# Gated experts summed in one running sum that VectorE finishes, with VectorE's step reordered and one norm fused

## What is computed

```python
# 1: top-k cross attention to a context (257 x 192), then a state-space layer and an MLP
scores = einsum(x @ Wq, ctx @ Wk) / sqrt(DH)          # 4 heads
topv, topi = top_k(scores, 32); attn = scatter(softmax(topv)); attn_mean = attn.mean(heads)
c_t = attn_mean @ (ctx @ Wv)
xf  = layernorm(x) * (1 + g * scale_in(c_t)) + g * shift_in(c_t)
y   = s4d(xf) * (1 + g * scale_out(c_t)) + g * shift_out(c_t)   # a long convolution
xt  = x + y
xt  = xt + gelu(layernorm(xt) @ W1 + b1) @ W2 + b2
x1  = x + layernorm(xt)
# 2: attention over the 32 rows
x2  = x1 + attention(layernorm(x1))
# 3: eight experts, top 2 of them gated
logits = cos_scores(h, centroids) + h @ w_route.T
gates  = softmax(top 2 of logits)
out    = x2 + sum_e gates[e] * (gelu(h @ w1[e] + b1[e]) @ w2[e]) + gates @ b2
```

## Time and profile before

| | |
|---|---|
| median of 3 runs | 602.14 us (600.91 to 603.63) |
| profiled execution, its own time | 601.02 us |
| its span, first to last instruction | 599.2 us |
| mean granted clock of PE | 0.972 |
| busy: PE, DVE, ACT, POOL | 550.1, 497.5, 292.6, 282.3 us |
| steps with all four tiles in work | some 31.6 us each |

### The profile page before, as it was taken

One profiled execution on the slowest core, in us unless ns is written; L12 is line 12 of the kernel. 1 busy time (PEld: TensorE's weight loads), 2 busy tenths in 40 slices (PEclk: granted clock), 3 DMA queues, 4 the chain that ended last, 5 costly groups with the idle time before them and its releaser, 6 DMA issues.

```text
span 599.2 us, 13091 instructions
## 1 busy us (share of the span) xinstructions
PE 550.1 (92%) x4558; PEld 406.0 (68%) x4558; DVE 497.5 (83%) x1761; ACT 292.6 (49%) x768; POOL 282.3 (47%) x662
## 2 busy tenths in 40 slices
PE   2588487999999999999999999999999999989877
PEld 2344264868686877778786868686868687766755
DVE  7997877689898999989899999898999899966433
ACT  3132242364646565555546463646464656434522
POOL 7755147525445362626363636353544535251621
PEclk9998898899999999999999999999999999989988
DMA  8488203030403030301213030303030300000000
GB/s 269 76 311 340 79 1 122 2 113 2 131 2 131 1 128 4 100 33 59 73 25 108 19 113 20 112 19 114 2 131 2 131 1 10 2 10 2 9 1 18
DMA packets 17957, 42.33 MB, mean 71 GB/s; under 512 B 2770, under 2 KB 9570, under 8 KB 17380
## 3 DMA queue, kind: packets, MB, share of 16 engines
q1 hardware_dynamic: 17892, 41.51, 20.7%
HBM read 39.37 MB, written 2.13 MB: 69 GB/s over the span
## 4 chain that ended last, share of the span: by engine, by line
PE 77%; DVE 3%; issue 3%; POOL 3%; ACT 2%; POOLq 0%; DVEq 0%
PE D L1136 9%; PE BB L1136 9%; PE BB L1159 8%; PE D L1153 8%; PE SS L1116 4%; PE SS L1122 3%; PE PC L1277 3%; PE PC L1316 2%; PE PC L1279 2%; PE BB L1237 2%; PE BB L1238 2%; PE BB L1272 2%; PE BB L1271 2%; PE PC L1219 2%; PE BB L1254 2%
## 5 line engine op out<-in xcount | busy, mean ns | idle before, releaser
L553 POOL TENSOR_SCALAR var_in<-mv 128x1 f32<-128x1 f32 x64 | 14.0, 219 | 238.4 <-DVE mv L782 140.9
L817 DVE MATCH_REPLACE8 work<-top,work 128x257 f32<-128x257 f32 x192 | 77.5, 412 | 0.0
L1136 PE MATMUL D<-ang,e_w 128*128 128x128 f32 x512 | 73.6, 292 | 0.0
L1136 PEld LDWEIGHTS D<-ang,e_w 128*128 128x128 f32 x512 | 65.6, 202 | 10.1 <-issue 10.1
L811 DVE MAX8 top<-work 128x8 f32<-128x257 f32 x192 | 71.1, 412 | 0.0
L1153 PE MATMUL D<-expw,ang 128*128 128x256 f32 x256 | 66.0, 389 | 1.2 <-ACT ang L628 0.9
L1136 PE MATMUL BB<-ang,w 128*128 128x128 f32 x512 | 65.0, 282 | 0.9 <-ACT ang L709 0.9
L1136 PEld LDWEIGHTS BB<-ang,w 128*128 128x128 f32 x512 | 62.1, 196 | 3.1 <-ACT ang L709 1.3
L628 ACT ACTIVATE ang<-BB,cols 128x128 f32<-128x128 f32 x128 | 36.5, 367 | 50.9 <-PE BB L1136 50.9
L1159 PE MATMUL BB<-expw,ang 128*128 128x256 f32 x256 | 57.9, 379 | 0.0
L649 ACT ACTIVATE expo<-SS,nmax,srs 128x257 f32<-128x257 f32 x64 | 32.7, 562 | 51.5 <-DVE work L797 51.3
(11 more groups left out here) (262 smaller groups left out, 1238.5 us busy)
## 6 DMA issues: line engine op xcount, KB each, us to landing
ctx_n<-in_ctx_n SPq DMA_DIRECT2D x16, 768.0 KB, 4.3
ctx_t<-in_ctxT SPq DMA_DIRECT2D x16, 514.0 KB
ctx_t<-in_ctxT SPq DMA_DIRECT2D x16, 257.0 KB
xT<-in_xT SPq DMA_DIRECT2D x16, 128.0 KB, 2.5
x_all<-in_x SPq DMA_DIRECT2D x4, 512.0 KB, 9.2
out<-out_sb SPq DMA_DIRECT2D x16, 128.0 KB, 1.7
ctx_l<-in_ctx_l SPq DMA_DIRECT2D x16, 96.0 KB, 5.1
w<-in_W SPq DMA_DIRECT2D x1, 1024.0 KB
```

The costliest lines, as they stand in the source:

```text
L817: V.match_replace(work[:, 2 * q + k, :], top[:, 2 * q + k, 8 * r8:8 * r8 + 8], work[:, 2 * q + k, :], TAKEN).then_inc(chains["taken"], 1)
L1136: ins = MM(bank[:, 128 * m:128 * m + 128], w[:, k, at:at + 128], xs[:, 128 * k:128 * k + 128], start=k == 0, stop=k == 1)
```

## The change

- `acc` is one buffer. Addition 0 adds the first product to x2, additions 1 to 7 add to `acc`, each of them waiting for the one before, and addition 8 writes `out_sb` itself, after a wait for the store that read it last. GpSimd's addition and its semaphore are gone; SP's store waits for DVE's ninth addition.
- The norm of tile c is two instructions: `u_c = (xt2 - mean) * g`, placed before rstd is there, and `x1 = u_c * rstd + xb_c`.
- On DVE many dependent instructions that stood next to each other now have an instruction of another tile between them. `find8`, `take8` and `probs` are split so that their halves can stand apart, and the nine gated additions stand one by one. PE's and ACT's programs are unchanged.

```diff
-        acc = [over("ang", D) for _ in range(2)]
+        acc = over("ang", D)
...
-                    wait(sp, s["fin_g"], dd.count(1, 1))
+                    wait(sp, s["acc_v"], dd.count(NE + 1, NE + 1))
...
-                if dd:
-
-                    wait(pool, s["acc_v"], dd.count(NE + 1, NE + 1))
-                    wait(pool, st_out[dd.p], dd.half(16, 0))
-                    nc.gpsimd.tensor_tensor(out_sb[dd.p][:, :], acc[0][:, :], acc[1][:, :], ALU.add).then_inc(s["fin_g"], 1)
...
+                        else:
+                            wait(dve, s["acc_v"], dd.count(NE + 1, k))
+                        if k < NE:
+                            so_far = acc if k else x2[dd.p]
+                            V.scalar_tensor_tensor(acc[:, :], bank, gate[:, k:k + 1], so_far[:, :], ALU.mult, ALU.add).then_inc(s["acc_v"], 1)
+                        else:
+                            wait(dve, st_out[dd.p], dd.half(16, 0))
+                            V.tensor_tensor(out_sb[dd.p][:, :], bank, acc[:, :], ALU.add).then_inc(s["acc_v"], 1)
...
+                if c:
+                    wait(dve, s["st1_v"], one(c))
+                    V.scalar_tensor_tensor(u_c[:, :], xt2[:, :], mv[1][:, 0:1], gout[:, :], ALU.subtract, ALU.mult).then_inc(chains["u"], 1)
...
+                    V.scalar_tensor_tensor(x1[:, :], u_c[:, :], rstd[1][:, 0:1], xb_c[:, :], ALU.mult, ALU.add).then_inc(s["x1_v"], 1)
...
                 if dd:
-                    gated(range(0, 2))
-                if a:
-                    take8(a, 0, 2)
-                if b:
-
+                    gated((0,))
+                if a:
+                    take8(a, 0, 2, (1,))
+                if dd:
+                    gated((1,))
+                if b:
                     wait(dve, s["y_a"], one(b))
                     wait(dve, s["y_mm"], one(b))
...
+                    V.tensor_tensor(yb[:, :], yb[:, :], B1[:, 0:D], ALU.mult).then_inc(chains["y"], 1)
+                if a:
+                    find8(a, 0, 3, (0,))
+                if b:
+                    wait(dve, chains["y"], b.count(2, 1))
+                    V.tensor_tensor(yb[:, :], yb[:, :], B1[:, D:2 * D], ALU.add).then_inc(chains["y"], 1)
+                if a:
+                    find8(a, 0, 3, (1,))
+                if b:
+                    wait(dve, chains["y"], b.count(2, 2))
                     wait(dve, s["xln_g"], one(b))
                     V.tensor_tensor(xt[:, :], yb[:, :], xln[b.n % 3][:, :], ALU.add).then_inc(s["xt_v"], 1)
+                if dd:
+                    gated((2,))
+                if b:
                     wait(dve, s["xt_v"], one(b))
                     link(V.bn_stats(bn[0][:, :], xt[:, :]))
                     V.bn_aggr(mv[0][:, :], bn[0][:, :]).then_inc(s["st0_v"], 1)
-                if a:
-                    find8(a, 0, 3)
...
                 if dd:
-                    gated(range(2, 4))
+                    gated((3,))
...
                 if dd:
-                    gated(range(4, 6))
+                    gated((4,))
                 if a:
                     take8(a, 0, 3)
+                if dd:
+                    gated((5,))
+                if a:
+                    find8(a, 1, 1)
                 if c:
                     wait(dve, s["o2_mm"], one(c))
                     V.tensor_tensor(x2[c.p][:, :], x1[:, :], C0[:, 0:D], ALU.add).then_inc(s["x2_v"], 1)
```

More of the change, by code:

```diff
@@ L274, in build @@
                  "xb_g x1_v st2_v rs2_g xl2_v xT2_mm xT2_a v_mm v_a s_mm nmaxc_v pc_a pt_v r_mm r_a o2_mm x2_v st3_v rs3_g inorm_g "
-                 "xl3_v xT3_mm xT3_a lg_mm dots_a nbest_v ed_a gate_v gT_mm gT_a e1a_mm e1b_mm g2a_a g2b_a eo_mm acc_v fin_g").split()
+                 "xl3_v xT3_mm xT3_a lg_mm dots_a nbest_v ed_a gate_v gT_mm gT_a e1a_mm e1b_mm g2a_a g2b_a eo_mm acc_v").split()
         s = {n: sem(n) for n in names}
-        chains = {n: sem("self_" + n) for n in "tm g0 g1 g2 g3 len top taken u xhat best".split()}
+        chains = {n: sem("self_" + n) for n in "tm g0 g1 g2 g3 len top taken u xhat best y gate bn2 bn3".split()}
         ld_x = [sem(f"ld_x{k}") for k in range(4)]
@@ L802, in top8, with find8 @@
                 take8(a, q, r8)
-            def find8(a, q, r8):
-                for k in range(2):
+            def find8(a, q, r8, ks=(0, 1)):
+                for k in ks:
                     if r8 == 1:
@@ L865, in step @@
                     V.tensor_tensor(xt2[:, :], xt_b[:, :], B1[:, 0:D], ALU.add).then_inc(s["xt2_v"], 1)
+                if b:
+                    sums(b, 1)
+                if c:
                     wait(dve, s["xt2_v"], one(c))
-                    stats(1, xt2[:, :], c, "st1_v")
+                    link(V.bn_stats(bn[1][:, :], xt2[:, :]))
+                    V.bn_aggr(mv[1][:, :], bn[1][:, :]).then_inc(s["st1_v"], 1)
                 if a and a.n == 3:
@@ L970, in step @@
                     V.tensor_tensor(x2[c.p][:, :], x1[:, :], C0[:, 0:D], ALU.add).then_inc(s["x2_v"], 1)
+                if a:
+                    prob_of(a, 0, 0)
+                if c:
                     wait(dve, s["x2_v"], one(c))
-                    stats(3, x2[c.p][:, :], c, "st3_v")
+                    V.bn_stats(bn[3][:, :], x2[c.p][:, :]).then_inc(chains["bn3"], 1)
                 if a:
-                    probs(a, 0)
-                    top8(a, 1, 1)
+                    prob_of(a, 0, 1)
+                if c:
+                    wait(dve, chains["bn3"], one(c))
+                    V.bn_aggr(mv[3][:, :], bn[3][:, :]).then_inc(s["st3_v"], 1)
+                if a:
+                    sums(a, 0)
                 if dd:
-                    gated(range(6, 8))
+                    gated((6,))
                 if a:
-                    top8(a, 1, 2)
+                    take8(a, 1, 1)
                 if dd:
-                    gated(range(8, NE + 1))
+                    gated((7,))
+                if a:
+                    find8(a, 1, 2)
+                if dd:
+                    gated((8,))
+                if a:
+                    take8(a, 1, 2)
                 if a and a.n == 1:
```

80 lines of the change are left out of this document (41 added, 39 removed).

## The result

| | before | changed |
|---|---|---|
| median, and range | 602.88 us (600.91 to 605.47, 4 runs) | 634.57 us (633.91 to 635.39, 4 runs) |
| profiled execution | 601.02 us | 633.91 us |
| its span | 599.2 us | 632.1 us |
| mean granted clock | 0.972 | 0.957 |

The ratio is 1.053, 95% interval 1.050 to 1.056: slower by 31.7 us, where 24.4 were forecast.

The account below looks back on a forecast made before the run. PE, full in 13 steps, was taken as the bound, with no margin to additions 4 and 5. 601.0 + 23.0 - 0.9 + 2.5 = 625.6 profiled, so median 626.5 us; range 609 to 638.

Parts of the forecast that it names:

- The early addition 2 and the replacements: DVE between xt and additions 4 and 5: PE stands 1.77 us longer in each of 13 steps, 23.0 us.
- The rest of the step: Interleaved small steps, running sum and tile c's norm inside the 13 steps: slack or hidden, no loss counted beyond the 1.77.
- the stop: PE's waits per step: about 0.3 before probability products, 0.4 before transposes of hn, 1.1 to 1.3 before the bias product.
- price nothing: Running sum in the steps: other work stands between the dependent additions, so their waits cost nothing.
- the chain worked out: From addition 2's start at 357.05 through statistics, hn, additions 4 and 5 to PE's bias product: 362.20 against 360.43.
- The start: First two steps, ahead of the 13: called latency, not throughput; the sum holds no term for them.
- The clock: PE's granted clock falls after the new stop in one or two of 13 steps: 2.5 us, bounds none and five (8.5).
- The tail: Steps after the 13, GpSimd's addition, norm, running sum and last tile b step together: -0.4 - 0.9 - 0.7 + 0.3 + 0.8 = -0.9 us.
- The last step with tile b: In the tail, no MATCH_REPLACE8 but the same wait: bias product at 552.54 against 551.72, 0.8 late.
- only the replacement counts: Rival: hn comes in its turn, only MATCH_REPLACE8 between additions 4 and 5 costs, 0.6 a step, 609 us; chance 0.06.
- DVE was the bound: Rival: DVE is the pacemaker and gets shorter, so the kernel is faster, 599 us; chance 0.05.
- The clock in every step: Rival: clock falls in all 13 steps, 13 x 1.7 = 22 on top of the stall, 647 us; chance 0.05.

Follow-up runs that it names:

- The two moves alone: Kernel before with addition 2 put between xt and its statistics and round 3's replacements between additions 4 and 5, nothing else: 627.73 us, ratio 1.041.
- The kernel with the filled stops: Changed kernel plus five unread 128x128 products on PE ahead of the bias product, in steps with a following tile: 629.61 us, ratio 1.047.
- its cure: Changed kernel with gated addition 2 back behind the row maximum of tile c, next to addition 3: 617.89 us, ratio 1.028.
- the profile with z moved: Changed kernel with product z put ahead of the two MAX8 of round 2, nothing else: 632.04 us, ratio 1.051.
- both moves undone, z early: Changed kernel with addition 2 back beside addition 3, replacements back behind addition 5, and z ahead of round 2's two MAX8: 608.37 us, ratio 1.007.

## Why the prediction was right, and where its sizes were off

The mechanism and its place were right, and the size was 7 short. By its steps:

- **The early addition 2 and the replacements.** Forecast 1.77 a step. The two moves alone give 33.39 - 31.60 = 1.79. Right. Within it, the products with the attention probabilities start only 0.1 late and not 0.2 to 0.3, the transposes of hn wait 0.38 (0.4) and the bias product 1.14 (1.1 to 1.3).
- **The rest of the step**, priced at nothing, is the term that was mis-sized. The step grew by 2.08, not 1.77, so 27.0 instead of 23.0 in 13 steps. Of the 0.31 too little, 0.24 is z (1.84 for the stop and 0.24 for z make 2.08): the forecast looked at the interleaved small steps only as fillers of gaps, but PE waits for z at once, and it was pushed behind two MAX8, on a DVE that comes there late from its wait of 1.3 for `xt_b`. The running sum costs 0.37 in the old order, where its additions are neighbours; the forecast took 0.13 for a dependent pair, and a pair measures 0.19 with a PSUM operand. In the changed order other work stands between them, and there the forecast's "price nothing" holds: the stop of 1.84 is 0.07 above the chain worked out, of which GpSimd's norm is the most (2.34 for 2.27).
- **The start**, priced at nothing, is the other. The first bias product of the 13 steps is at 145.72 instead of 139.11, 6.6 later, 2.1 of it the step itself. For the rest, the clock in the stretch 20 to 45 us is the most visible difference, the first row of before and the second of the changed kernel:

```profile
20.00:45.00 25.00, 17.56 (x86) 8.44 (x94) 24.66 (x58) 6.57 (x16) 15.78 (x17) 0.96 0.75 218
```

```profile
20.00:45.00 25.00, 18.92 (x42) 8.22 (x42) 24.66 (x62) 4.70 (x10) 12.69 (x12) 0.66 0.78 234
```

  The kernel with the fused norm alone, whose start has nothing new in it before tile c, has 0.66 in this stretch too, and its first bias product at 142.10. The kernel with the filled stops has 0.81 there, and reaches the transposes of hn ahead of its first filled stop at 141.69, where the changed kernel, whose program is the same up to there, is at 144.14. So some 2.5 to 3 us differ from one execution to another. The remaining 1.5 to 2 were not traced to their end.
- **The clock.** Forecast one or two falls in the steps at 1.7, so 2.5; the profile has two at 1.4 in the 12 steps, 2.8, and a third behind the last stop, in the tail. The sum came out close, each fall was priced too high, and which stops they follow stays open.
- **The tail.** Forecast -0.9; from the last bias product of a full step to the end it is 79.2 for 80.7, so -1.5, although its first step has two falls worth 2.6, where before it had one. The last step with tile b is as forecast: addition 2 starts at 583.41 and the bias product at 588.05, 4.64, where the forecast's chain gives 4.50. But the clock moves the tail by more than the forecast's terms. The three steps of the tail before, and of the changed kernel:

```profile
518.50:551.70 33.20, 29.34 (x226) 22.27 (x225) 22.39 (x76) 14.92 (x40) 12.61 (x34) 0.95 0.01 5
551.70:576.90 25.20, 22.37 (x172) 18.73 (x172) 10.36 (x34) 11.55 (x32) 9.21 (x25) 0.93 0.02 7
576.90:594.80 17.90, 13.15 (x62) 11.08 (x62) 6.84 (x20) 4.84 (x14) 4.66 (x13) 0.81 0.02 7
```

```profile
552.90:588.05 35.15, 30.93 (x226) 23.35 (x226) 20.47 (x72) 14.53 (x38) 12.33 (x33) 0.90 0.01 4
588.05:611.30 23.25, 20.68 (x172) 17.43 (x172) 10.16 (x33) 11.24 (x30) 8.80 (x24) 1.00 0.02 7
611.30:628.30 17.00, 12.01 (x62) 9.78 (x62) 6.82 (x20) 4.67 (x14) 3.94 (x12) 0.90 0.02 8
```

  Clock times length gives 6.8 us of full clock missing before and 5.2 after. The second step got 1.95 shorter, and its clock went from 0.93 to 1.00: up to 1.8 of that is the clock, so whether the norm's 0.9 and the other terms add up can't be read here. Single rows show the norm's saving (0.83) and, for the running sum, six dependent additions in a row at the end.

In sum: 12 steps of 2.08 and the one in the start make 27.0, two falls in the steps 2.8, the rest of the start 4.5, the tail -1.5: 32.8 of the span's 32.9. Of the rivals, "only the replacement counts" falls: the wait for hn is there, and its cure is worth 0.83 a step (33.68 to 32.85). "DVE was the bound" falls by the running sum alone, where DVE has less to do and the kernel is slower. "The clock in every step" falls: it was three of 13, though five in the profile with z moved, with the same stop.

The measured 634.57 lies high in the range of 609 to 638. With no fall of the clock the forecast's own bounds end at 602.1 + 28.6 - 0.9 = 629.8: the room left for up to five falls held what z and the start added, so that the range held is in part luck. Two slips in its sums are small: 625.6 and 1.1 make 626.7, not 626.5, and 1.5 us a step without falls gives 620.7, not 619.

## What to carry to other kernels

In a stream that runs in order, an instruction moved up to fill a gap brings its own wait with it, and all that stands behind pays for it: look up when its input is ready, not only where the gap is. Count backwards from the engine that is full: only instructions ahead of one of its waits matter there, so a change that makes DVE 19 us shorter can be worth nothing, and 0.4 us of work put ahead of such a wait costs 0.4 in every step. Two sums that join in idle time avoid the dependence that one sum has at each addition.

## What the hardware showed unexpectedly

- A dependent pair of 128x256 additions with one operand in PSUM starts 0.58 apart, 0.39 without the dependence (1.06 against 0.87 for the pair). Six of them in a row at the end of the changed kernel take 3.43:

```profile
625.99 3.43 DVE L844 SCALAR_TENSOR_TENSOR ang<-D,gate,ang 128x256 f32<-128x256 f32 x6 [0.55 <-PE D L1186]
```

- Behind an idle time of 1.13 of PE, itself behind a shorter one of 0.38 (1.89 us busy in the 3.40 shown), the clock halved in some steps and not in others, with the same rows around it. With the 1.13 filled by products it halved behind none of 12.
- One kernel (both moves undone, z early) has times in two groups, five around 601.9 and seven around 610.1, with granted clocks of 0.982 in the faster and 0.958 to 0.972 in the slower. The clock goes with it, but what picks the group stays open.
